# Smaller scratch for the dynamic gathers, and more buffers of gathered rows in both layers of a graph network

## What is computed

```python
# layer one (4 heads of 32)
feat_self, feat_nei = relu(x @ W0 + b0), relu(x @ W1 + b1)          # [N, 128] each
edge_w = (att_s[row] + att_n[col]) * adj_vals                       # row = src, col = dst
agg    = segment_sum(edge_w * feat_nei[col], row)
x = layernorm(x + concat(norm(feat_self), norm(agg)))
# layer two
messages = relu(concat(x[src], x[dst]) @ W_msg + b_msg)             # [E, 256]
agg = segment_sum(messages, dst)
x = layernorm(x + layernorm(relu(concat(x, agg) @ W_upd + b_upd)) * gamma + beta)
```

## Time and profile before

| | |
|---|---|
| median of 3 runs | 5591.37 us |
| time of the profiled execution | 5593.93 us |
| span of its core in the profile | 5592.4 us (1.5 us lie around it) |
| first gather of layer one to the last | 687 to 3073 us |
| first gather of layer two to the last | 3119 to 5523 us |
| VectorE busy over the span | 64% |
| ScalarE busy over the span | 45% |
| bytes moved by DMA | 711 MB, of which 435 MB by GpSimd's queue |

### The profile page before, as it was taken

How to read it: one execution, slowest core, us unless ns; L and a number is a source line. 1 busy time by engine, 2 the same in 40 slices (tenths; PEclk the granted TensorE clock), 3 DMA queues, 4 the chain that set the end, 5 groups by cost and what they waited for, 6 DMA issues and landing times.

```text
span 5592.4 us, 75218 instructions
## 1 busy us (share of the span) xinstructions
PE 3788.5 (68%) x21392; PEld 2980.5 (53%) x21392; DVE 3562.9 (64%) x8129; ACT 2532.8 (45%) x6368; POOL 3351.4 (60%) x3403
## 2 busy tenths in 40 slices
PE   0998645665666566656656577777777777777775
PEld 0898634444444444444444465556565556655654
DVE  4999845555555555555555366666666666666665
ACT  0674333333333333333333355555555555555554
POOL 2333366666666666666666466666666666666663
PEclk9999878777878878777778788889888888899898
DMA  3330134444444444444444455555555555555554
GB/s 98 97 96 13 29 113 127 129 130 125 132 126 129 129 129 128 132 124 129 130 126 117 110 147 151 150 147 152 147 154 149 150 150 148 152 147 153 149 152 92
DMA packets 393093, 711.08 MB, mean 127 GB/s; under 512 B 77542, under 2 KB 233410, under 8 KB 392654
## 3 DMA queue, kind: packets, MB, share of 16 engines
q0 software_dynamic: 161104, 434.80, 28.3%
q1 hardware_dynamic: 231582, 271.44, 16.0%
HBM read 622.28 MB, written 85.27 MB: 127 GB/s over the span
## 4 chain that ended last, share of the span: by engine, by line
PE 29%; DVE 24%; another core or an unknown queue 20%; issue 15%; ACT 6%; DVEq 3%; POOL 2%; DMA 1%; SPq 0%; ACTq 0%; POOLq 0%
PE ps L1092 9%; PE ps L1103 8%; DVE big L1565 6%; DVE big L1430 6%; PE ps L1070 4%; ACT arena L830 4%; DVE arena L1575 3%; POOL arena L675 2%; DVE big L1351 2%; PE ps L1058 2%; PE ps L1009 2%; PE ps L965 1%; PE ps L1121 1%; DVEq L1565 1%
## 5 line engine op out<-in xcount | busy, mean ns | idle before, releaser
L687 POOL DMA_INDIRECT arena<-d_p,tabS x1628 | 1563.0, 960 | 887.7 <-issue 462.5
L675 POOL DMA_INDIRECT arena<-d_t,tabD x1628 | 1563.5, 960 | 822.7 <-issue 448.5
L1070 PE MATMUL ps<-arena 128*128 128x256 f32 x3256 | 1012.0, 466 | 923.4 <-DVE big L1430 403.1
L1070 PEld LDWEIGHTS ps<-arena 128*128 128x128 f32 x3256 | 724.2, 233 | 1138.9 <-DVE big L1430 725.0
L1092 PE MATMUL ps<-arena 128*128 128x256 f32 x3256 | 951.0, 432 | 292.4 <-DVE big L1565 191.5
L1103 PE MATMUL ps<-big,tabE 128*128 x3256 | 877.6, 411 | 312.4 <-DVE arena L1575 212.0
L1575 DVE TENSOR_TENSOR arena<-arena,ps 128x512 f32<-128x512 f32 x814 | 533.2, 683 | 702.9 <-remote 422.1
L1092 PEld LDWEIGHTS ps<-arena 128*128 128x128 f32 x3256 | 660.6, 214 | 528.4 <-ACT arena L932 192.3
L932 ACT ACTIVATE arena<-arena 128x1024 f32<-128x1024 f32 x407 | 430.1, 1057 | 1087.8 <-DVE arena L1575 915.5
L1103 PEld LDWEIGHTS ps<-big,tabE 128*128 128x128 f32 x3256 | 663.8, 207 | 459.0 <-issue 355.6
L1565 DVE SCALAR_TENSOR_TENSOR big<-big,tabK,ps 128x256 f32 x1628 | 775.5, 476 | 99.5 <-issue 44.3
(11 more groups left out here) (249 smaller groups left out, 3738.3 us busy)
## 6 DMA issues: line engine op xcount, KB each, us to landing
arena<-d_loc SPq DMA_DIRECT2D x407, 256.0 KB
arena<-d_t,tabD POOLq DMA_INDIRECT x1628
arena<-d_p,tabS POOLq DMA_INDIRECT x1628
arena<-in_xT_dram SPq DMA_DIRECT2D x96, 256.0 KB
d_t<-arena SPq DMA_DIRECT2D x49, 256.0 KB, 2.2
d_xp<-arena SPq DMA_DIRECT2D x49, 256.0 KB
arena<-d_xp SPq DMA_DIRECT2D x49, 256.0 KB
d_x<-arena SPq DMA_DIRECT2D x49, 256.0 KB
```

What stands on the lines that cost most here:

```text
L675: e.indirect_dma_start(out=GB[g][:, k, :], out_offset=None, in_=d_t, in_offset=bass.IndirectOffsetOnAxis(ap=tabD[:, j, k:k + 1], axis=0)). ...
L687: e.indirect_dma_start(out=G1[j % 8][:, k, :], out_offset=None, in_=d_p, in_offset=bass.IndirectOffsetOnAxis(ap=tabS[:, j, k:k + 1], axis= ...
L1070: m = e.matmul(PS[4 + 2 * q + k // 2][:, (k % 2) * 256:(k % 2) * 256 + 256], OH[q][:, k, :], GB[(g - 1) % 4][:, k, :], start=True, stop=True)
```

## The change

- The kernel is built with `dynamic_dma_scratch_size=4096`. `arena` grows by 3072 words (12288 bytes) in each partition.
- Layer one has six buffers of gathered rows (`EB` = 6) in place of four, and the wait of POOL goes from `e_d` at j - 3 to j - 5.
- Layer one has four one-hots in place of two. VectorE makes that of group j + 1 in step j (in step 0 those of groups 0 and 1), after a wait for `e_d` at n - 3 for group n. The wait for `e_d` at j - 1 now stands behind the one-hot, ahead of the additions only.
- Layer two has ten buffers of gathered rows (`FB` = 10) in place of eight, and the wait goes from 2(j - 7) to 2(j - 9).
- Semaphores and the places of some temporary arrays follow.

```diff
-AW = 12032
+AW = 15104
+EB = 6
+FB = 10
@@ carving of arena
-        OH = [take(4, 128) for _ in range(2)]
-        GB = [take(4, 256) for _ in range(4)]
+        OH = [take(4, 128) for _ in range(4)]
+        GB = [take(4, 256) for _ in range(EB)]
...
-        G1 = [take(4, 256) for _ in range(8)]
+        G1 = [take(4, 256) for _ in range(FB)]
+        take = carve(A, 10752)
@@ gpsimd
             def gath0(j, g, i):
-                waitn(e, "e_d", j - 3)
+                waitn(e, "e_d", j - EB + 1)
...
             def gath(j, g, i):
-                waitn(e, "f_ag", 2 * (j - 7))
+                waitn(e, "f_ag", 2 * (j - FB + 1))
@@ vector, edge0
-                waitn(e, "e_d", j - 1)
-                if not done(j, NG):
-                    e.tensor_tensor(OH[g % 2], ..., ALU.is_equal).then_inc(S("e_oh"), 1)
+                for n in ((0, 1) if j == 0 else (j + 1,)):
+                    if n < NG:
+                        waitn(e, "e_d", n - 3)
+                        e.tensor_tensor(OH[n % 4], ..., ALU.is_equal).then_inc(S("e_oh"), 1)
                 if p2:
+                    waitn(e, "e_d", j - 1)
                     for k in range(4):
@@ build
-    nc = _bacc.Bacc("TRN2", target_bir_lowering=False, num_devices=1)
+    nc = _bacc.Bacc("TRN2", target_bir_lowering=False, num_devices=1, dynamic_dma_scratch_size=4096)
```

More of the change, by code:

```diff
@@ L78 @@
 SHARED.update({"g_" + n: ("b_" + m, 2 * NP) for n, m in (("n1", "nm"), ("b1", "bn"), ("a1", "ag"))})
-SHARED.update({f"f_g{g + 4}": (f"e_g{g}", 64 * ((NG - g + 3) // 4)) for g in range(4)})
+SHARED.update({f"f_g{g + 4}": (f"e_g{g}", 64 * ((NG - g + EB - 1) // EB)) for g in range(EB)})
 SHARED.update({"ump": ("u0p", 2 * 1600), "u1p": ("e_d", NG), "ufp": ("tp", 3 + len(TABE)), "umv": ("tb", T_DONE), "u_w": ("u_l", 96)})
@@ L355, in gnn @@
         wB = take(1600)
-        take = carve(A, 7680)
+        take = carve(A, 10752)
         gR = take(NC, 256)
-        take = carve(A, 7680)
+        take = carve(A, 10752)
         edge = take(NC, 128)
         past = b16(take(NC * 64))
-        take = carve(A, 11008)
+        take = carve(A, 14080)
         sli = take(512).bitcast(i32)
@@ L676, in gath0 @@
                                          in_offset=bass.IndirectOffsetOnAxis(ap=tabD[:, j, k:k + 1], axis=0)).then_inc(S(f"e_g{g}"), 16)
-            drive(e, NG, 4, gath0)
+            drive(e, NG, EB, gath0)
             stored_own(e)
@@ L684, in gath @@
             def gath(j, g, i):
-                waitn(e, "f_ag", 2 * (j - 7))
+                waitn(e, "f_ag", 2 * (j - FB + 1))
                 for k in range(4):
-                    e.indirect_dma_start(out=G1[j % 8][:, k, :], out_offset=None, in_=d_p,
-                                         in_offset=bass.IndirectOffsetOnAxis(ap=tabS[:, j, k:k + 1], axis=0)).then_inc(S(f"f_g{j % 8}"), 16)
-            drive(e, NG, 4, gath)
+                    e.indirect_dma_start(out=G1[j % FB][:, k, :], out_offset=None, in_=d_p,
+                                         in_offset=bass.IndirectOffsetOnAxis(ap=tabS[:, j, k:k + 1], axis=0)).then_inc(S(f"f_g{j % FB}"), 16)
+            drive(e, NG, FB, gath)
             finished(e)
@@ L826, in edge0 @@
                 if not done(j, NG, 1):
-                    q = (g - 1) % 4
-                    waitn(e, f"e_g{q}", 64 * uses(i, g, 1, 4))
+                    q = (j - 1) % EB
+                    waitn(e, f"e_g{q}", 64 * ((j - 1) // EB + 1))
                     for k in range(4):
@@ L931, in _ @@
                     waitn(e, "f_m", 2 * (g + 1))
-                    e.activation(G1[g % 8], G1[g % 8], ACT.Relu).then_inc(S("f_re"), 1)
+                    e.activation(G1[g % FB], G1[g % FB], ACT.Relu).then_inc(S("f_re"), 1)
         @block.tensor
@@ L1070, in edge0 @@
                         m = e.matmul(PS[4 + 2 * q + k // 2][:, (k % 2) * 256:(k % 2) * 256 + 256],
-                                     OH[q][:, k, :], GB[(g - 1) % 4][:, k, :], start=True, stop=True)
+                                     OH[(j - 1) % 4][:, k, :], GB[(j - 1) % EB][:, k, :], start=True, stop=True)
                     m.then_inc(S("e_d"), 1)
@@ L1092, in edge1 @@
                             m = e.matmul(turn(H, AB)[:, k * 256:k * 256 + 256], OH1[(j - 2) % 4][:, 2 * h + k, :],
-                                         G1[(j - 2) % 8][:, 2 * h + k, :], start=True, stop=True)
+                                         G1[(j - 2) % FB][:, 2 * h + k, :], start=True, stop=True)
                         m.then_inc(S("f_ag"), 1)
```

8 lines of the change are left out of this document (4 added, 4 removed).

## The result

The changed kernel takes 5646.39 us (median of 4 runs, 5642.26 to 5650.68), the kernel before in the same comparison 5592.43 us (4 runs). The ratio is 1.0094, 95% interval [1.0077, 1.0112]: slower by 54 us, where 36 us less had been forecast. The time lies above the range of 5400 to 5630.

The account below looks back on a forecast made before the run. No engine was full; POOL's gather streams held back the PE counts that release POOL, setting the cycle. Gains of 26 + 0 + 8 = 34 us off 5593.93 gave 5560, or 5557 for the median; range 5400 to 5630.

Parts of the forecast that it names:

- the time with no pause left: Both layers: taking POOL's 753 us of waits for free buffers from 5594 us leaves 4841 us.
- The length of a cycle: POOL's streams and pauses: each cycle takes about 1.41 us per gather plus 0.5 us, which longer streams spread.
- the far end of my range: Gather stretches: all streams as cheap as the one of 32, 5.66 us a group, saving 80 and 102 us.
- Six buffers, 26 us: Layer one: relieving streams of four and used-up buffers takes a group from 5.86 to 5.79 us, 26 us gained.
- One-hots ahead: DVE, layer one: wait moves behind the one-hot, additions start 0.69 us sooner; at most 104 us, counted inside the 26.
- Ten buffers in layer two, 0 us: Layer two: rows are never late with eight buffers, so 5.91 us a group stays; ends 0 and 102 us.
- The signs that I had named: If right: layer one pauses fall about 30 us, few streams of four stay, gathers keep 0.96 us.
- Rival (1): No difference: PE alone sets stream length, buffers only shift POOL; 5583 to 5600 us, chance 0.23.
- rival (2): Long streams: deeper buffers let POOL run on, 5.66 us a group in both layers; 5401 us, chance 0.15.
- The edges, -8 us: Layer ends: last gathers start two groups earlier, 12 us, with two more groups behind; 4 us gained per layer.
- The scratch, 0 us: Dynamic gathers' scratch cut from 16384 to 4096 bytes: counted as no cost, its ends left to the rivals.
- rival (3): Slower: POOL's gathers wait for room in the scratch; 5612 us, or 6008 with costly laps, chance 0.17.

Follow-up runs that it names:

- Job A: Kernel before with scratch 4096 alone, and the changed kernel with single parts put back, in a job without pauses: 4886.28 to 4887.96 us, kernel before 4891.12 us.
- first profile: Profiled executions of the kernel before, 5593.93 us, and of the changed kernel, 5650.68 us, both with pauses.
- e13: Kernel before with three buffers of rows in layer one and six in layer two, scratch 16384, with pauses: 5549.59 us, 0.9995.
- E: Job with pauses, kernel before 5552.35 us: fewer buffers 0.9995, gathers spaced by a fill 0.9966.
- e14: Kernel before with a 128 x 200 fill on GpSimd behind each gather, with pauses: 5531.28 us, 0.9966.
- e16: Kernel before with gathers of 64 rows instead of 128 behind the first buffers' worth, with pauses: 5600.28 us, 1.0019.
- F: Job with pauses, kernel before 5590.84 us: changed kernel with layer two at eight buffers 1.0074, kernel before with half the rows 1.0019.
- e5: The whole change again, against the kernel before in a job with pauses: 5600.69 us, 1.0098.
- B: Job with pauses, kernel before 5550.57 us: the whole change 1.0098, the scratch alone 1.0057.
- e6: Kernel before with scratch 4096 and nothing else, in a job with pauses: 5578.05 us, 1.0057.
- e15: Changed kernel with layer two back at eight buffers, against the kernel before in a job with pauses: 5630.01 us, 1.0074.
- e19: Kernel before with scratch 2048 and nothing else, in a job without pauses: 1.0001.
- e18: Kernel before with scratch 4096 and the arena at its new length of 15104 words, in a job without pauses: 0.9987.
- first comparison: Changed kernel against the kernel before, four runs each, with pauses: 5646.39 us against 5592.43 us, 1.0094.
- e1: Kernel before with scratch 4096 and nothing else, in a job without pauses: 4887.21 us, 0.9995.

## Why the prediction was wrong

*Where the kernel waits.* Right: groups of four paced at 5.86 and 5.91 us, pauses of POOL, counts of PE that arrive together once POOL is still. Job A shows the other side of it: without held counts the time is 4891 us, near the 4841 that I had worked out as the time with no pause left (a gather behind a pause shows no 0.30 us of issue, so the sum took some 70 us too many out of the stretches; shorter edges give a part back). What I did not know is that this was a property of the runs I looked at and not of the kernel.

*The length of a cycle.* This step failed first. I took 1.41 us for each gather and 0.5 us for each cycle, and drew gain from spreading the 0.5 us over longer streams. From the starts of the gathers, over streams of 12 and more with the pause behind them (a pause is 0.8 us and more of idle time; the first stream of each layer is left out), layer one and layer two:

| kernel (job) | scratch | us per gather |
|---|---|---|
| before (first profile) | 16384 | 1.447, 1.466 |
| e13, fewer buffers (E) | 16384 | 1.431, 1.453 |
| e14, spaced (E) | 16384 | 1.444, 1.463 |
| e16, half the rows (F) | 16384 | 1.436, 1.462 |
| changed (first profile) | 4096 | 1.453, 1.482 |
| e5, changed (B) | 4096 | 1.441, 1.471 |
| e6, scratch alone (B) | 4096 | 1.439, 1.470 |
| e15, layer two at eight (F) | 4096 | 1.457, 1.480 |

In layer one of the changed kernel streams of 12 and of 16 both take 5.81 us a group, and in e14 streams of 68 are no cheaper than streams of 16, though its own spacing hides most of what could be gained. From 12 gathers on there is nothing left to spread, and what the few streams of four cost (6.44 us a group in layer one) is all that ever was to be had, 39 x 0.65 = 25 us. The stream of 32 at the head of layer two (5.66 a group), from which I took the far end of my range, starts with nothing queued behind POOL and so, I take it, is no measure of a steady state. With ten buffers POOL issued 44 gathers to the first long pause, 3145.18 to 3207.67 us, 5.68 a group: no less than the 32.

*Six buffers, 26 us.* No gain. e13 with three has the time of four (0.9995); six without the small scratch weren't run in a job with pauses, but e5, which has them beside e6, is 7.6 us longer in layer one and not shorter. That "the number sets only how far ahead POOL stands" was in my own text, and that half was right; the exception that I made for the streams of four was not. They went from 39 to 51, so they don't come from want of buffers. *One-hots ahead.* The wait moved as forecast (779.4 us at the one-hot to 71.9 there and 918.0 at the additions), and nothing was gained. *Ten buffers in layer two, 0 us.* Right: e5 and e6, in one job, have 1.471 and 1.470 us a gather there. The signs that I had named said as much: pauses 20 us up in place of 30 down, more streams of four in place of few, gathers at 0.96 us. Rival (1), that buffers only shift POOL, was right on the buffers; rival (2) needs longer streams to be cheaper, and neither the streams of 12 and 16 nor those of e14 are.

*The edges, -8 us.* Wrong in sign. I let POOL's last gather start two groups earlier because POOL stands further ahead. But POOL's own rate is the limit, so that gather starts no earlier, and two more groups lie behind it. In the jobs with pauses it is 39.1 us between the layers with three buffers, 40.3 to 47.0 with four and 51.0 to 54.4 with six; the drain is 61.8 to 70.1 with six and eight and 75.9 and 77.9 with ten. With the first gather, the gap and the drain the edges cost 14 us in place of giving 8. In jobs without pauses they don't (37.4 to 40.3 us between the layers with four buffers, 37.3 to 38.0 with six): there the consumers keep up.

*The scratch, 0 us.* The largest miss, a term that I put at nothing because no row showed a cost. Alone it costs 0.57%, 32 us on 5551 (27 us by the medians). My ends for it were long gathers and waits for room, rival (3). The rival had the sign and a time (5612) nearer the truth than the forecast, but not the mechanism, so that is luck: gathers stay at 958 ns, and the time went into the pauses. Nor is room in the scratch what they wait for: from 3145.18 to 3194.08 us the changed kernel issued 40 gathers 1.25 us apart, while TensorE had finished with two groups (L1095 at 3162.84 and 3175.92). So 32 stood unfinished and no gather waited, which is more than the 28 that I had estimated for 4096 bytes.

In the table the smaller scratch takes 0.006 us per gather more in layer one and 0.016 in layer two in the first pair of profiles, 1628 x 0.022 = 36 us, the size of the 32 us measured, though that pair differs in the buffers too. Across jobs the same holds where the kernel before takes alike (e13 against e6, 5552 and 5551): 0.008 and 0.017. By whole stretches e6 is 21.0 us longer than e13 in layer two and 0.3 us shorter in layer one; whether it costs anything in layer one is therefore open.

How a smaller scratch lengthens the pauses isn't shown: whether by its size, or because another scratch size moves the tiles to other places, no run tells apart. Still smaller sizes weren't tested with pauses. From the 9 descriptors on each engine that the Trainium skill states ("DMA: Bandwidth & Descriptors", The descriptor swizzle) my estimate was room for 28 gathers in 4096 bytes and, by the same sum, 14 in 2048. If that room is right, the 32 unfinished gathers above say that it is given back by landings and not by buffers. e19 says little on it: there POOL seldom stood more than 14 gathers ahead of what TensorE had done (2% of the gathers of layer two, none of layer one).

The sum, redone: scratch 32 us (e6), edges about 20 (14 in the first pair, 20 of the 31.6 us between e5 and e6), the buffers and one-hots in the stretches 0 to 12. That is 52 to 64 us against 54. Of these the scratch's share is shown by one job with pauses (e6), that fewer buffers change no rate is shown (e13), the edges are read from traces and not isolated (e15 leans that way), and whether the tiles' new places add something wasn't decided (e18 fell in a job without pauses).

## What to carry to other kernels

A rate hides behind a wait: where an engine stops and goes, divide whole cycles by what is done in them, for short and long cycles apart, before crediting anything to more room. If the quotient stays the same, room buys nothing; fewer instructions of the kind that is rated might, which wasn't tried here. An edit "at no cost" needs a run of its own, above all a change of a resource that no row shows. And see a kernel in a second job before explaining its pauses: here the same program took 4899 us in one job and 5551 us in another on the same chip.

No version is the one to take in both kinds of job. The spaced one gains 0.34% with pauses and loses 10% without.

## What the runs showed of the hardware

- With gathers of GpSimd issued on end, TensorE's counts arrived within 0.1 us of its modelled end in four jobs. In the other three, and in the first comparison, they came late: there up to 13.3 us in the kernel before and 23.5 us in the changed one, while the waits for ScalarE and VectorE in the kernel before ended within 0.52 us. The time is the same for all runs of a job within 0.7%, and differed between two jobs on one chip (4899 and 5551 us for one program). What sets it stays open.
- In the jobs with late counts 1.43 to 1.48 us pass for each gather over a stream and its pause, and this doesn't fall with half the rows (1.0019), nor clearly with spacing (5.78 and 5.84 us a group, e13 5.84 in both).
- With 4096 bytes of scratch 40 gathers were issued 1.25 us apart, 32 of them into buffers that TensorE hadn't finished with (3145.18 to 3194.08 us of the changed kernel).
- A fill of 0.12 us between two gathers costs nothing (1.0011): it fits in the 0.30 us that POOL spends on issue. One of 0.28 us costs 0.15 us.
- The granted clock was higher where TensorE was held up less: 0.86 and 0.97 in the two layers of e1, 0.79 and 0.88 in the earlier trace rows.
